# Two attention layers on one core: scores before the shift by maxima, zero products on TensorE until operands land, halved first loads, PSUM claimed pair by pair, and a new order of all steps

## What is computed

```python
# layer 0: queries = x, keys = values = ctx
Q = relu(x @ Wq.T + bq); K = relu(ctx @ Wk.T + bk); V = relu(ctx @ Wv.T + bv)
scores = einsum('bqd,bkd->bqk', heads(Q), heads(K)) / sqrt(16)      # causal, key mask
x = layer_norm(merge(softmax(scores) * query_mask @ heads(V)) + x)
# layer 1
n = layernorm1(x); q, k, v = heads(split(n @ sa_wqkv))
result = x + merge(softmax(causal(q @ k.T / 16)) @ v) @ sa_wproj + sa_bproj
k2, v2 = heads(split(layernorm2(ctx) @ ed_wkv)); q2 = heads(layernorm2(result) @ ed_wq)
result = result + merge(softmax(q2 @ k2.T / 16) @ v2) @ ed_wproj + ed_bproj
result = result + relu(layernorm3(x) @ ff_w1 + ff_b1) @ ff_w2 + ff_b2
```

## Time and profile before

| | us |
|---|---|
| median of 3 runs | 385.3 (382.94 to 386.32) |
| the profiled execution, its time | 384.1 |
| its span, first to last instruction | 382.3 |
| PE busy | 341.8 |
| DVE busy | 226.6 |
| ACT busy | 172.5 |
| POOL busy | 53.2 |

### The profile page before, as it was taken

One profiled execution on the slowest core, in us unless ns is written; L12 is line 12 of the kernel. 1 busy time (PEld: TensorE's weight loads), 2 busy tenths in 40 slices (PEclk: granted clock), 3 DMA queues, 4 the chain that ended last, 5 costly groups with the idle time before them and its releaser, 6 DMA issues.

```text
span 382.3 us, 9700 instructions
## 1 busy us (share of the span) xinstructions
PE 341.8 (89%) x4144; PEld 261.7 (68%) x4144; DVE 226.6 (59%) x558; ACT 172.5 (45%) x297; POOL 53.2 (14%) x67
## 2 busy tenths in 40 slices
PE   7888699998999999998999999879989989887894
PEld 4666589886867777766668777655968757575663
DVE  5398997746657639564487545838943263645212
ACT  3346654465570263914326144655464535211551
POOL 2014141041320010120211012240100211000000
PEclk9999989999999999999999999999999999999999
DMA  7684103000000100000000020000000000000001
GB/s 223 186 328 137 63 2 104 3 2 2 25 2 0 45 40 24 3 2 2 24 6 3 0 82 2 3 0 26 3 2 2 2 2 2 3 0 0 3 2 48
DMA packets 4260, 13.43 MB, mean 35 GB/s; under 512 B 525, under 2 KB 1669, under 8 KB 3962
## 3 DMA queue, kind: packets, MB, share of 16 engines
q1 hardware_dynamic: 3928, 12.72, 10.0%
q10 hardware_dynamic: 290, 0.10, 0.1%
HBM read 11.89 MB, written 0.92 MB: 34 GB/s over the span
## 4 chain that ended last, share of the span: by engine, by line
PE 69%; DVE 16%; ACT 8%; issue 6%; ACTq 0%; DVEq 0%
PE ring L493 34%; PE ring L740 7%; DVE negmax L1021 7%; ACT exps L848 6%; PE ring L754 4%; PE ring L619 4%; PE ring L599 4%; PE ring L593 3%; PE acc L644 3%; PE ring L631 3%; DVE negmax L1000 3%; PE ring L663 2%; PE ring L611 1%; PE ring L705 1%; PE ring L525 1%
## 5 line engine op out<-in xcount | busy, mean ns | idle before, releaser
L1021 DVE TENSOR_REDUCE negmax<-ring 112x2 f32<-112x750 f32 x64 | 57.1, 936 | 42.2 <-PE ring L740 42.1
L848 ACT ACTIVATE exps<-ring 125x896 f32<-125x896 f32 x48 | 41.4, 914 | 43.7 <-PE ring L754 43.5
L1232 POOL TENSOR_SCALAR_AFFINE_SELECT exps<-exps 112x896 f32<-112x896 f32 x32 | 31.4, 1007 | 130.9 <-ACT exps L848 130.9
L1000 DVE TENSOR_REDUCE negmax<-ring 112x8 f32<-112x896 f32 x32 | 33.4, 1086 | 17.9 <-PE ring L599 17.7
L644 PE MATMUL acc<-exps,v 125*17 125x112 f32 (+1 forms) x1280 | 39.4, 264 | 0.8 <-ACT v L825 0.4
L644 PEld LDWEIGHTS acc<-exps,v 125*17 125x17 f32 (+1 forms) x1280 | 28.7, 98 | 13.8 <-issue 10.2
L848 ACT ACTIVATE exps<-ring,pad 112x896 f32<-112x896 f32 x32 | 30.5, 1004 | 16.7 <-PE ring L631 16.7
L740 PE MATMUL ring<-k,q 32*112 32x376 f32 x256 | 28.8, 517 | 10.2 <-DVE negmax L1021 6.0
L493 PE MATMUL ring<-w_b,h 128*112 128x256 f32 x128 | 29.5, 383 | 0.0
L619 PE MATMUL ring<-maxrows,sel 32*125 32x224 f32 (+1 forms) x320 | 19.1, 310 | 10.8 <-issue 2.9
L882 ACT ACTIVATE h<-ring,flat_c 128x224 f32<-128x224 f32 x32 | 11.7, 449 | 34.4 <-PE ring L493 34.4
(11 more groups left out here) (143 smaller groups left out, 552.1 us busy)
## 6 DMA issues: line engine op xcount, KB each, us to landing
c_nat<-in_ctx SPq DMA_DIRECT2D x4, 750.0 KB
w_b<-in_w_b SPq DMA_DIRECT2D x1, 2304.0 KB, 10.2
xk_t<-in_xk_t SPq DMA_DIRECT2D x4, 448.0 KB, 4.1
w_a<-in_w_a SPq DMA_DIRECT2D x1, 1280.0 KB, 5.7
xh<-in_keys SPq DMA_DIRECT2D x4, 224.0 KB, 2.8
x_nat<-in_x SPq DMA_DIRECT2D x4, 224.0 KB, 4.0
out<-x SPq DMA_DIRECT2D x4, 224.0 KB, 2.4
w_qk<-in_w_qk SPq DMA_DIRECT2D x1, 512.0 KB, 4.7
```

The costliest lines, as they stand in the source:

```text
L848: return nc.scalar.activation(exps[0:k, EXP_AT[job], :, :], o[0:k, :, 0:4 * T], ACT.Exp, bias=bias)
L1000: v_max[b].step(nc.vector.tensor_reduce(negmax[0][:, slot(g, b), 2 * m_:2 * m_ + 2, :], o[0:T, :, 0:4 * T].rearrange("p r (j t) -> p r j t ...
L1021: x_max[b].step(nc.vector.tensor_reduce(negmax[1][:, b, 2 * m_:2 * m_ + 2, i], o[0:T, :, 0:S], AX.X, ALU.max, negate=True), g, 2 * i + m_ + 1)
L1232: p_masked[b].step(nc.gpsimd.affine_select(e, e, [[0, 8], [1, T]], ALU.is_ge, 0.0, base=0, channel_multiplier=-1), g, k)
```

## The change

- X and cX: the scores' products go first and open the banks; then PE waits for `maxrows` and adds the shift. The signals that the banks are full move to the last of the shift's products.
- `quad` claims a pair only when the first product for it is issued. All four kinds of quad use it.
- PE begins with `keep_busy(10)`: ten bf16 products of 128 x 128 by 512 columns of zeros into a ring bank, after a first DVE memset of their operand `idle`.
- The first loads are halved: x part, q0 weights, keys part, k0 weights, with a semaphore for each; later groups' x and keys parts are two DMAs too, each with its own wait.
- PE's waits for the masks are for the steps of `keys` that it needs instead of for all.
- t2 and y are done for each batch, each in one bank (`SMALL`), with the ACT copy, the DVE addition and the store for each batch (8 stores of 112 KB instead of 4 of 224 KB). Stream Y is gone; the steps stand at the end of streams B and F.
- `MIX` is new, 323 steps. It begins rows(0), q0(0), flag, k0(0), rows(1), where it was rows(0), rows(1), flag, q0(0), k0(0). It ends ... cX(3,1,2), cV(3,1,1), t2(3,0), cV(3,1,2), y(3,0), cO(3,1), f(3,1), t2(3,1), y(3,1), where it was ... cX(3,1,2), cV(3,1,1), cV(3,1,2), cO(3,1), y(2), t2(3), y(3).

```diff
-    return [("cS", g, b, i) for i in range(4)] + [("cM", g, b), ("cX", g, b, 0), ("cX", g, b, 1), ("cV", g, b, 0), ("cX", g, b, 2), ("cV", g, b, 1), ("cV", g, b, 2), ("cO", g, b)]
+    return [("cS", g, b, i) for i in range(4)] + [("cM", g, b), ("cX", g, b, 0), ("cX", g, b, 1), ("cV", g, b, 0), ("cX", g, b, 2), ("cV", g, b, 1), ("cV", g, b, 2), ("cO", g, b), ("t2", g, b), ("y", g, b)]
...
-           "F": [x for g in GROUPS for x in b_steps(g, 1)], "Y": [(n, g) for g in GROUPS for n in ("t2", "y")],
+           "F": [x for g in GROUPS for x in b_steps(g, 1)],
...
-MIX = ("RRLAANLNCNEDECDNCPAJCWNCWDEPIWDJINDPIJCIPDCDPIAJPAAIAJHJCJIHDEPCDPCEPEDCIDCDPJEAJIPAJAHAPINAAFIFJBPIJBKBABEPCHBNEBABPFBF"
-       "EPBBFCEFNEFPEPDNBCKBBFBCBEBFFDBPFIFKYDYFDFCDBKDCDBCBBPJABANAFPCAPDPCDBJCEFCDFIPDCDBPAFAANFFFAFJAIFBFBYPIBYFJBIJPHHBJIPIJ"
-       "BPBFEBBEEPJPIHIJEIBJBFIFJIJBEFEFEKEFEFFFBFBBFKFBHBPBFKFBBFBFBBYFKBFFFFFFYYY")
+MIX = ("RALARLNNDENCAECDCPNWDEPIJPCNCWDDWPIJINCJDCDIPIAJPAIAAJDHJCHCDIJPEPCPEEDCJDCDPIEPAHIJAAJPPAIAANFIFJBIJBKBABPCPBNFEFNBEBBB"
+       "FEBEDNBFPBFBFDFCBEDFPBFBFPNABCKFBFFPCFDCDEHBCDCPBDEBAPFPAAFDECBBPCDFBDBCAFDNIDBCJPCBFAFIJIAFAFIFPAJAKFBPBFKBFBJBIJPHHBJI"
+       "JPIBPEBBEBEFHJBIHJIEJPBIJFFIJIFBKEBFEEFPBEFEFFBFBFBFBKFBBFFBKFFBBFBBFFPBFFFFBFBFKFF")
...
-SMALL = ("counts", "M", "O", "cM", "cO", "f")
+SMALL = ("counts", "M", "O", "cM", "cO", "f", "t2", "y")
...
+        idle = acc_sb[2][:, :, :].rearrange("p s t -> p (s t)")[:, 0:256]
...
+            for part in range(2):
+                load_x(0, part)
+                sp.dma_start(w_qk0[:, part, :, :].rearrange("p c u -> p (c u)"), w_d["qk0"][:, part * C * U:(part + 1) * C * U]).then_inc((q0_loaded, k0_loaded)[part], 16)
+            sp.wait_ge(xq_loaded[0], 16)
...
             def quad(step):
 
-                pair = [claim(pe, step + (m,)) for m in range(2)]
-                return [pair[r // 2][:, r % 2, :] for r in range(R)]
+                pairs = {}
+
+                def bank(r):
+                    if r // 2 not in pairs:
+                        pairs[r // 2] = claim(pe, step + (r // 2,))
+                    return pairs[r // 2][:, r % 2, :]
+                return bank
...
-                        nc.tensor.matmul(bank[r][0:k, 2 * c * T:2 * (c + 1) * T], sel[rows, c:c + 1].to_broadcast([32, k]), maxrows[i][rows, :], start=c == 0, stop=False, skip_group_check=True)
+                        m = nc.tensor.matmul(bank(r)[0:k, 2 * c * T:2 * (c + 1) * T], sel[rows, c:c + 1].to_broadcast([32, k]), maxrows[i][rows, :], start=False, stop=c == C - 1, skip_group_check=True)
+                        if c == C - 1 and r % 2:
+                            end(m)
...
             def self_shifted(g, l, b):
                 bank = quad(("X", g, l, b))
-                pe.wait_ge(*a_m[b].at(g, l + 1))
-                minus_max(bank, slot(g, b), T)
                 for c in range(C):
                     for r in range(R):
                         rows = slice(32 * r, 32 * r + 32)
-                        m = nc.tensor.matmul(bank[r][0:T, 2 * c * T:2 * (c + 1) * T], kf[g % 2][rows, c, b, :],
-                                             qf[g % 2][rows, c, b, :, :].rearrange("p e t -> p (e t)"), start=False, stop=True, skip_group_check=True)
-                        if c == C - 1 and r % 2:
-                            end(m)
+                        nc.tensor.matmul(bank(r)[0:T, 2 * c * T:2 * (c + 1) * T], kf[g % 2][rows, c, b, :],
+                                             qf[g % 2][rows, c, b, :, :].rearrange("p e t -> p (e t)"), start=c == 0, stop=False, skip_group_check=True)
+                pe.wait_ge(*a_m[b].at(g, l + 1))
+                minus_max(bank, slot(g, b), T)
...
-            def out2_transposed(g):
-                rows_transposed(("t2", g), o_nat[1], lambda b: pe.wait_ge(*x_o[b].done(g)))
+            def out2_transposed(g, b):
+                o = claim(pe, ("t2", g, b))
+                pe.wait_ge(*x_o[b].done(g))
+                for c in range(C):
+                    m = nc.tensor.transpose(o[:, 0, c * T:(c + 1) * T], o_nat[1][:, b, c * 128:(c + 1) * 128], ident[0:T, 0:T])
+                end(m)
...
-            def project_y(g):
-                pe.wait_ge(*a_ot[1].done(g))
-                tokens_out(("y", g), lambda b: token_pairs(o_t[1], b, wf["wp2"]))
-
+            def project_y(g, b):
+                o = claim(pe, ("y", g, b))
+                pe.wait_ge(*a_ot2[b].done(g))
+                end(products(token_pairs(o_t[1], b, wf["wp2"]), o[0:T, 0, 0:U]))
+
+            def keep_busy(n):
+
+                for _ in range(n):
+                    nc.tensor.matmul(ring[2][:, 1, :], idle.bitcast(BF16)[:, 0:128], idle.bitcast(BF16), start=True, stop=True, skip_group_check=True)
+
+            pe.wait_ge(prep_dve, 1)
+            keep_busy(10)
...
-            def result(g):
-                o = is_filled(dve, ("y", g))
-                for b in range(G):
-                    dve.wait_ge(*v_f[b].done(g))
-                v_res.step(nc.vector.tensor_tensor(x1[g % 2][:, :, :], o[0:T, :, 0:U], x1[g % 2][:, :, :], ALU.add), g, 1)
+            def result(g, b):
+                o = is_filled(dve, ("y", g, b))
+                dve.wait_ge(*v_f[b].done(g))
+                v_res[b].step(nc.vector.tensor_tensor(x1[g % 2][:, b, :], o[0:T, 0, 0:U], x1[g % 2][:, b, :], ALU.add), g, 1)
```

More of the change, by code:

```diff
@@ L407, in _, with load_x @@
         def _(sp):
[L408 removed]
+            def load_x(g, part):
                 if g > 1:
[L410 to L413 removed]
+                    if part == 0:
+                        sp.wait_ge(*a_q0.done(g - 2))
+                    else:
+                        sp.wait_ge(*a_k0.done(g - 2))
+                        sp.wait_ge(*v_v0.done(g - 2))
+                sp.dma_start(xk_t[g % 2][:, part, :, :, :].rearrange("p c b t -> p (c b t)"), xk_t_d[g][:, part * C * G * T:(part + 1) * C * G * T]).then_inc((xq_loaded, xk_loaded)[part][g % 2], 16)
             def load_queries(g):
@@ L480, in next_queries @@
                     load_queries(g + 2)
-            run({"general": general, "xqT": lambda g: load_keys(g + 2) if g + 2 < NG else None, "v0": lambda g: load_x(g + 2) if g + 2 < NG else None, "cT": lambda g, b: next_context(g) if b == G - 1 else None, "xT": next_queries, "y": store})
+            run({"general": general, "xqT": lambda g: load_keys(g + 2) if g + 2 < NG else None, "v0": next_x, "cT": lambda g, b: next_context(g) if b == G - 1 else None, "xT": next_queries, "y": store})
             for i in range(2):
-                sp.wait_ge(stored[i], 16 * (NG // 2))
+                sp.wait_ge(stored[i], 16 * G * (NG // 2))
         @block.tensor
@@ L739, in cross_scores @@
                     rows = slice(32 * r, 32 * r + 32)
-                    m = nc.tensor.matmul(bank[r][0:T, 0:SP], q2[g % 2][rows, c, b, e, :], k2[g % 2][rows, b, c, :], start=True, stop=True)
+                    m = nc.tensor.matmul(bank(r)[0:T, 0:SP], q2[g % 2][rows, c, b, e, :], k2[g % 2][rows, b, c, :], start=True, stop=True)
                     if r % 2:
@@ L748, in cross_shifted @@
                 bank = quad(("cX", g, b, ch))
-                pe.wait_ge(*c_m[b].done(g))
-                minus_max(bank, 4 + b, CH)
                 for c in range(C):
@@ L753, in cross_shifted @@
                         rows = slice(32 * r, 32 * r + 32)
-                        m = nc.tensor.matmul(bank[r][0:CH, 2 * c * T:2 * (c + 1) * T], k2[g % 2][rows, b, c, ch * CH:(ch + 1) * CH],
-                                             q2[g % 2][rows, c, b, :, :].rearrange("p e t -> p (e t)"), start=False, stop=True, skip_group_check=True)
-                        if c == C - 1 and r % 2:
-                            end(m)
+                        nc.tensor.matmul(bank(r)[0:CH, 2 * c * T:2 * (c + 1) * T], k2[g % 2][rows, b, c, ch * CH:(ch + 1) * CH],
+                                             q2[g % 2][rows, c, b, :, :].rearrange("p e t -> p (e t)"), start=c == 0, stop=False, skip_group_check=True)
+                pe.wait_ge(*c_m[b].done(g))
+                minus_max(bank, 4 + b, CH)
             def cross_sum(g, b, ch):
@@ L1164, in weights_lo @@
                 nc.vector.scalar_tensor_tensor(wkv2[:, LO, i, :], unsplit[:, i, :], vec[:, VEC["g2"] + i:VEC["g2"] + i + 1], wkv2[:, HI, i, :].bitcast(F32), ALU.mult, ALU.subtract).then_inc(split_lo, 1)
+            nc.vector.memset(idle, 0.0).then_inc(prep_dve, 1)
             nc.vector.memset(ones_row[:, :], 1.0).then_inc(prep_dve, 1)
```

74 lines of the change are left out of this document (37 added, 37 removed).

## The result

The changed kernel takes 375.2 us (374.5 to 376.0), the kernel before beside it 385.8: a ratio of 0.974, 95% interval 0.969 to 0.979, so 10 us less where 4.3 were forecast. The same kernel measured again beside the last experiments (e13) has a ratio of 0.979 (0.976 to 0.982), 8.0 us less. So the gain is some 8 to 10 us. The profiled execution has a span of 373.3 us (before 382.3).

A forecast was written before the change was run, and what follows sets the result against it. TensorE's program order was taken to set the time, with only its idle time or slow work to win. Start -1.9, early order -2.1, middle +2.0, end -2.3 made -4.3 us: 381.0 us, 8-in-10 range 374.5 to 388.

The forecast's parts named there:

- finer claims: Quads claiming pair by pair: an early first half ends nothing earlier for PE, so no gain was counted.
- scores first: X and cX: scores ahead of the wait for maxrows cover at most 0.8 us; value 0.3, inside the other middle gaps.
- start: Zero products, halved loads and q0 ahead end the first self scores at 14.7 instead of 16.6: -1.9 us.
- new order, early and middle: Order of steps: -2.1 us up to xT(0), +2.0 from 55.13 to 370, where more steps wait for a pair.
- end: Last steps by batch: shorter y(3,1), add and copy, waits covered by y(3,0) and t2(3,0); -2.3 us.
- A half costs the whole: In cS, two row groups take near 0.90 us, as a whole quad does; the other bound was 0.45.
- Rival 1: A half costs half (0.45 us), saved at each of 13 places: middle -3.9, in all -10.2, time 375.1; chance 0.22.
- rival 2: Start: the zero products do not lift the clock; +0.6 instead of -1.9, time 383.5; chance 0.14.
- rival 4: The start's gain is given back at DVE, busy early: -1.9 and -2.1 shrink to -1, time 384; chance 0.10.
- Slow stretch gone: Early order: the slow-clock stretch at 46.79 to 50.40 disappears because k2 fills PE's waits; 1.8 us.
- 13 places: Steps after xT(0) claiming a pair under one eviction after its filling, against 10 in the old order: +3.5 us.
- the sign that I had named: Middle: gaps before cS and cX vanish but a waiting cS takes 1.9 us from first to last instruction.

The follow-up runs named there:

- e5: The kernel before with pairwise claims alone, shift still first: 375.1 us, ratio 0.976.
- e6: The kernel before with scores first alone, a quad still claiming both pairs at once: 384.3 us, ratio 0.998.
- e7: The kernel before with the start of the change alone: 384.9 us, ratio 1.000.
- e16: The changed kernel in the old order of steps and with the old start, keeping pairwise claims, scores first and the end by batch: 374.1 us, ratio 0.973.
- e11: The changed kernel in the old order of steps, with its start, pairwise claims, scores first and the end by batch: 373.3 us, ratio 0.970.
- e14: The same code as e11 (changed kernel in the old order of steps), measured again beside the last experiments: 373.3 us, ratio 0.970.
- e8: Start, pairwise claims and scores first on the old order, without the new order and the output projection by batch: 374.4 us, ratio 0.975.
- e1: The changed kernel with pairwise claims undone, so a quad claims both pairs before its first product: 393.3 us, ratio 1.021.
- e10: The kernel before with pairwise claims everywhere, but VectorE waits for the second half of a cS before evicting the first: 379.0 us, ratio 0.985.
- e15: e14 with VectorE waiting for the second half of a cS before it evicts the first: 376.7 us, ratio 0.980.
- e2: The changed kernel with the shift first again in X and cX, pairwise claims kept: 377.3 us, ratio 0.981.
- e12: e11 with rows(1), the second spread product, moved behind the first S: 372.8 us, ratio 0.970.
- e3: The changed kernel without its ten zero products: 378.7 us, ratio 0.981.
- e4: The kernel before, with its own order, start and end, plus pairwise claims and scores first: 376.5 us, ratio 0.976.

## Why the prediction was right and wrong

| term | forecast | measured, by |
|---|---|---|
| finer claims | 0 | -9.4 (e5) |
| scores first | -0.3, inside the middle | -0.7 (e6) |
| start | -1.9 | 0 (e7), -1.2 (e16) |
| new order, early and middle | -2.1 and +2.0 | +1.7 (first measurement, e11), +3.5 (e13, e14) |
| end | -2.3 | -2.1 by the ratios, -1.0 by the medians (e8, e11) |
| sum | -4.3 | -7.6 to -11.7; measured -8.0 to -9.9 |

Finer claims, scores first and the end are measured in the old order; new order and end are differences of kernels that have pairwise claims. In the new order the claims are worth 16 to 18 us (e1), so without them the new order would cost some 11 us, not 2 to 3.5 (an estimate: e1's 393.3 less the 382 that 384.6, e6's -0.7 and the end's -2.1 make).

**Finer claims: the step that failed.** "A half costs the whole" was right. The trace after has it:

```profile
344.76 1.56 PE L757 MATMUL ring<-k,q 32*112 32x376 f32 x12
345.70 3.48 DVE L1051 TENSOR_REDUCE negmax<-ring 112x2 f32<-112x750 f32 x4 [0.40 <-PE ring L757]
346.69 0.89 PE L757 MATMUL ring<-k,q 32*112 32x376 f32 x4 [0.37 <-DVE negmax L1051]
...
350.65 0.89 PE L757 MATMUL ring<-k,q 32*112 32x376 f32 x4 [0.38 <-ACT exps L875]
```

Four instructions, half a quad, take 0.89 us, as long as eight, behind a wait of 0.37 or 0.38. Wrong was what I concluded: "a first half that starts early ends nothing earlier for PE". It ends 0.1 us earlier, since a second half gets going 0.05 us after the release and a whole quad 0.15. At the waits of a full eviction the gain was no more than that (0.1 to 0.2 us each), but there are 52 waits of 0.12 us and over, and I had put the term at nothing. I then said of the evicting engine that behind a cS it gains nothing, "since DVE is then still busy with the old one (evictions of 0.94 us back to back)". The earlier trace rows gives no such thing: 936 ns is the mean of one eviction, and the same row has 42.2 us of DVE waiting for PE. The timeline shows DVE idle 0.23 us in each round. And I priced only the gaps of 0.85 us and over; the 42 waits under 0.6 us hold as much again, 11.4 us, and there pairwise claims break the taking of turns (8.0 us of the gain in the table above). The sum of PE's waits for cS in the earlier trace rows, 6.0 us in 14 and 3.6 in 8, longest 1.1, says by its mean of 0.4 that most are short. e10 and e15 give the share of DVE's earlier beginning at cS, 3.4 to 3.6 us of the time. Rival 1 gave 375.1, which is the measured time, but by a mechanism that the row above rules out: a half did not cost half.

**Scores first** had the right size, within an interval of -1.5 to +0.1 us.

**Start.** The products behaved as forecast: zero products 3.79 us, rows(0) 0.69, q0 and k0 1.78 each at the fast level, so rival 2 falls. In four other profiles with this start (e1, e2, e13, e15) all ten zero products ran slowly (4.45 us) and the fast level came only behind them, by up to 0.6 us; q0 took 1.78 us there too. Timeline of PE after:

```profile
1.26 3.79 PE L813 MATMUL ring<-acc_sb 128*128 128x512 bf16 x10 [1.26 <-DVE acc_sb L1195]
4.98 0.69 PE L577 MATMUL ring<-exps,ones_row 1*125 1x256 f32 x2
5.60 1.78 PE L503 MATMUL ring<-xk_t,w_qk 128*128 128x224 f32 x8
...
8.09 0.18 PE L586 MATMUL acc<-ones,first_masked 8*1 8x1 f32 x2 [0.71 <-DVE first_masked L1217]
...
13.43 0.59 PE L610 MATMUL ring<-mask_c,add_mask 112*112 112x448 bf16 x2 [0.49 <-ACT rows_sb L838]
13.95 1.41 PE L616 MATMUL ring<-kf,qf 32*112 32x112 f32 x32
15.29 3.05 PE L503 MATMUL ring<-xk_t,w_qk 128*128 128x224 f32 x8
```

The first self maxima began at 15.4, not at 14.7 (before 16.6). Missing in the sum were the 0.71 us wait for the flag's operand, and the slow stretch from 14.5 to 17.9, in which q0(1) takes 3.05 us for the 1.78 of the earlier trace rows. So PE's second projection ends near where it ended before, and e7 shows nothing left of the start. That is the first half of rival 4, the start's gain given back before the middle; whether DVE takes it back, as rival 4 has it, isn't shown (e12's maxima began 2.3 us earlier, and nothing came of it).

**Early order.** The transposition of normed rows stands at 53.7 after (forecast 51, before 55.1), but at 55.1 in e13, the same kernel, whose slow stretch was twice as long. With the old order it stands at 53.0 and 53.4 (e11, e14). So the new order gives nothing here. What the old order has over before comes where claims and start are together: the start alone has 54.6 (e7), claims and scores first with the old start 55.1 (e16), all with a slow stretch of 3.4 us. "Slow stretch gone" was wrong: it moved to 14.5.

**Middle.** The order was forecast at +2.0 from 13 places, with -2.1 early. I had the sign of the middle from the count of places, and e13/e14 bear it out: +3.5 for the whole order. The places were right as well. The ten cS among them take 1.6 to 2.1 us from the first to the last instruction in the trace after, all other cS at most 1.3 (346.7 and 350.7 are second halves of two of them). That is the sign that I had named for the forecast's step against rival 1. The early gain was not there.

**The end** came about as worked out: y(3,1) is four products (1.09 us for 1.98) and the last add is half as long. Timeline after:

```profile
365.12 3.62 PE L503 MATMUL ring<-w_b,h 128*112 128x256 f32 x16
...
368.97 0.36 ACT L899 ACTIVATE o_t<-ring 128x224 f32<-128x224 f32 x1 [4.56 <-PE ring L796]
369.47 1.09 PE L503 MATMUL ring<-w_b,o_t 128*112 128x256 f32 x4 [0.54 <-ACT o_t L899]
...
370.60 0.42 DVE L1189 TENSOR_TENSOR x<-ring,x 112x256 f32<-112x256 f32 x1 [1.40 <-PE ring L503]
```

From the end of the add to the end of the span it is 2.3 us (2.85 before), the half microsecond that I had left open. From the last exponential to the end of the span it is 10.1 us, 6.5 without f(3,1), where my sign said 8: it forgot that y(2), 1.9 us, leaves this stretch.

## What to carry to other kernels

When a producer and a consumer share a ring, price a finer claim by the whole loop, not by one step: if the row of the consumer shows a wait for the producer inside a burst, and the producer one for the consumer, they take turns, and letting the producer begin in what is free pays in every round, even where a half costs as much as the whole. Add up the many waits of 0.2 us before pricing the few of 1 us: the few stay nearly as long as they were. What a wait costs beyond the release (here 0.15 us for an idle engine, 0.05 for one at work on the same quad) is paid at every one of them. A new order made together with a part should be tried without it and the part without the order: here the order without the part was slower than the kernel before (e1), and the part was better without the order (e11).

## What the runs showed of the hardware

Ten zero bf16 products of 128 rows brought the fast level: in the changed kernel the granted clock rises at 4.24, 3.0 us after they began, and each product goes from 0.43 to 0.22 us. In the ten profiles with them it rises 2.7 to 5.1 us after they began (e14 and e2). 5.5 us of one-row products had not done it. The Trainium skill, "TensorE: Matmul & The Clock Gate", Part 1, says that activity releases the slow default; for dense products these runs agree, for one-row products (5.5 us without a pause) they don't.

The fast level didn't stay. In 14 of the 16 profiles of experiments (not in e3 and e5) and in both of the two kernels a slow stretch of some 3 us or more lies in the first 60 us, at 14.5 in the changed kernel, at 47 before, at 25 to 30 in e16, and between 60 and 360 us there is one in e1 alone. The shortest are 3.4 us long. In e4 it lasted from 43.9 to 54.1, and the fast level is back within the second row (windows view: stretch, us, busy PE, PEld, DVE, ACT, POOL, granted clock, DMA, GB/s):

```profile
45.00:50.00 5.00, 5.00 (x52) 3.79 (x48) 4.63 (x14) 2.29 (x3) 2.65 (x3) 0.50 0.15 46
50.00:55.00 5.00, 5.00 (x47) 4.56 (x39) 4.09 (x10) 1.53 (x3) 3.17 (x4) 0.59 0.02 3
```

PE is busy all of it, at 1.2 GHz where the clock column says 0.50. A stretch of 3.4 us costs about 1.7 (an estimate: half of it), and two profiles of one kernel differ in it: e13's zero products took 4.45 us and its q0(1) 3.36, ending at 19.8; in the first profile of the same kernel these were 3.79 and 3.05, ending at 18.3. At the transposition of normed rows the two are 1.4 us apart (55.1 and 53.7), e4 and e5 4.0 (57.3 with the stretch of 10 us, 53.3 with none). So a difference of a few us between two single profiles shows nothing by itself. What brings the stretches back isn't shown by any run here.
